# Output product of the second attention from rounded parts: three one-pass matmuls per product, in groups of two turns

## The reference, cut to what matters

```python
q, k, v = hidden @ Wq.T, hidden @ Wk.T, hidden @ Wv.T      # 32 heads of 64
q, k = apply_rope(q, k, pos, pos)
out_local  = sliding_window_attention_blockwise(q[:, :30], k[:, :30], v[:, :30], 128)
out_global = global_attention(q[:, 30:], k[:, 30:], v[:, 30:])
out = jnp.concatenate([out_local, out_global], axis=1)      # (B, L, 2048)
return jnp.einsum('blp,hp->blh', out, Wo) + bo              # Wo: 256 x 2048
```

## Time and profile before

| | |
|---|---|
| median of three runs | 3144.66 us |
| span of the profiled execution | 3149.4 us |
| second attention in it | about 1626 us to the end |
| TensorE busy over the span | 3012.4 us (96%) |
| VectorE, ScalarE, GpSimd busy | 2118.6 (67%), 1863.2 (59%), 1017.1 us (32%) |
| output product, L1961 | 1024 MATMUL rows, 241.6 us busy |
| mean granted TensorE clock | 0.987 of full speed |

### The profile page before, as it was taken

How to read it: one execution, slowest core, us unless ns; L and a number is a source line. 1 busy time by engine, 2 the same in 40 slices (tenths; PEclk the granted TensorE clock), 3 DMA queues, 4 the chain that set the end, 5 groups by cost and what they waited for, 6 DMA issues and landing times. The chain is left out here.

```text
span 3149.4 us, 66407 instructions
## 1 busy us (share of the span) xinstructions
PE 3012.4 (96%) x23638; PEld 2264.0 (72%) x23638; DVE 2118.6 (67%) x5888; ACT 1863.2 (59%) x4638; POOL 1017.1 (32%) x1627
## 2 busy tenths in 40 slices
PE   7999999999999999997988999999999999999998
PEld 5888888853444444434877888788887888788886
DVE  5666666678989989975655555655556555555556
ACT  4666666647877778773445555455554555455553
POOL 0000000001100000001016666576656666566663
PEclk9999999989999999998999999999999999999999
DMA  4111111232333232103224444344443444244432
GB/s 150 50 48 48 48 48 41 60 68 44 69 50 64 35 75 45 30 9 116 83 69 110 99 101 94 103 122 101 94 107 93 114 103 95 67 114 105 102 87 68
DMA packets 296707, 246.35 MB, mean 78 GB/s; under 512 B 149180, under 2 KB 231740, under 8 KB 296252
## 3 DMA queue, kind: packets, MB, share of 16 engines
q1 hardware_dynamic: 296380, 242.11, 31.7%
HBM read 100.71 MB, written 44.04 MB: 46 GB/s over the span
## 5 line engine op out<-in xcount | busy, mean ns | idle before, releaser
L1838 ACT ACTIVATE b_pp<-b_pp,b_nm 128x192 f32<-128x192 f32 (+2 forms) x1024 | 472.8, 463 | 447.6 <-DVE b_nm L2005 366.1
L1007 ACT ACTIVATE a_pt<-ps 128x512 f32<-128x512 f32 x1024 | 556.1, 595 | 178.9 <-PE ps L1043 177.9
L176 DVE TENSOR_REDUCE mx<-ps 128x2 f32<-128x1024 f32 x512 | 622.3, 1224 | 58.6 <-PE ps L167 44.0
L1808 POOL TENSOR_SCALAR b_pp<-b_pp,b_rc 128x192 f32<-128x192 f32 x960 | 389.2, 428 | 383.9 <-DVE b_rc L2014 383.9
L2026 DVE COPY b_pt<-ps 128x384 f32<-128x384 f32 (+2 forms) x336 | 182.1, 556 | 316.7 <-PE ps L1927 301.4
L2005 DVE CUSTOM_DVE_ANT_0 b_pp<-ps,b_mk 128x192 f32<-128x192 f32 x960 | 276.3, 354 | 136.8 <-PE ps L1906 136.8
L797 DVE SCALAR_TENSOR_TENSOR f_yac<-ps,f_cw,f_yac 128x128 f32<-128x128 f32 x992 | 278.1, 344 | 125.3 <-PE ps L596 123.0
L596 PEld LDWEIGHTS ps<-w,f_sq 128*128 128x128 f32 x2048 | 265.2, 191 | 26.5 <-issue 6.0
L596 PE MATMUL ps<-w,f_sq 128*128 128x128 f32 x2048 | 270.2, 275 | 0.3
L1961 PE MATMUL ps<-b_wo,b_oT 128*128 128x256 f32 x1024 | 241.6, 380 | 3.7 <-ACT b_vv L1831 3.7
L1056 PE MATMUL ps<-a_pt,a_v 128*32 128x256 f32 x3072 | 242.0, 395 | 0.0
(11 more groups left out here) (282 smaller groups left out, 7332.8 us busy)
## 6 DMA issues: line engine op xcount, KB each, us to landing
b_rt<-b_qf SPq DMA_DIRECT2D x1024, 64.0 KB, 2.0
qk_parts<-f_aa SPq DMA_DIRECT2D x32, 512.0 KB, 2.7
v_rows<-f_va_ SPq DMA_DIRECT2D x16, 512.0 KB, 2.8
rl<-in_W1qT SPq DMA_DIRECT2D x64, 128.0 KB, 2.6
rl<-in_W1kT SPq DMA_DIRECT2D x64, 128.0 KB, 2.7
rl<-in_W1vT SPq DMA_DIRECT2D x32, 256.0 KB, 3.2
b_wo<-in_W1oT SPq DMA_DIRECT2D x16, 512.0 KB, 4.2
b_vs<-b_vv SPq DMA_DIRECT2D x60, 128.0 KB, 2.9
```

The lines of the kernel that those rows point to most:

```text
L176: e.tensor_reduce(M["mx"][kh % 3][:, :, jt, h], P.pair(s), AX.X, ALU.max, negate=True).then_inc(P.free_sem(s), 1)
L1007: e.activation(pt[(4 * i + 2 * j + a) % 12][:, :], P.ap((*s, a)), ACT.Exp).then_inc(P.free_sem((*s, a)), 1)
L1808: m = e.tensor_scalar(x, x, r[:, 2 * u + h:2 * u + h + 1], 1.0, ALU.mult, ALU.mult)
L1838: e.activation(x, x, ACT.Exp, bias=nm[n % 4][:, c:c + 1], scale=-1.0, accum_out=sm[n % 4][:, c:c + 1]).then_inc(exp_done, 1)
```

## The change

The attention rows `oT` (fp32) are replaced by a high part `oh` (fp32r, written by ScalarE in `evac`) and a low part `ol` (fp32r, written by VectorE in the new step `evac_low`, which now frees bank 7). The output weights are loaded raw (`wr`) and split into `woh` (ScalarE) and `wol` (GpSimd) in the new step `wo_split`. A product is three fp32r matmuls by `mm3` in place of one fp32 product. A group is two turns in place of four (`PB` = 8 groups a batch), so there are 32 groups and 256 `out` steps, and two of them are taken at the end of a local stride (one after every second whole stride). All pending `store` steps are put out together, ahead of the next `out` steps. The build call also sets `dynamic_dma_scratch_size` to 1024.

```diff
             if evacs and (u == 2 or len(slots) < 3):
                 out += evacs
-                evacs = []
             if u < len(turned):
                 out.append(turned[u])
+            if evacs and (u == 2 or len(slots) < 3):
+                out += [("evac_low", f[1]) for f in evacs]
+                lowered.update(evacs)
+                evacs = []
...
-            if store:
-                p.append(store.pop())
-            if side and (not last or j % 2):
+            p += store
+            store = []
+            for _ in range(min(len(side), j % 2 if last else 2)):
                 p.append(side.pop(0))
-                if p[-1][1] % 4 == 3:
+                if p[-1][1] % PB == PB - 1:
                     store.append(("store", *p[-1][1:]))
-        if at % 4 == 3:
-            p.append(("wo", n // 4))
-            side += [("out", n // 4, t) for t in range(NQ)]
+            if at % 2 and j == 0:
+                p.append(("wo", n // 2))
+        if at % 2:
+            p.append(("wo_split", n // 2))
+            side += [("out", n // 2, t) for t in range(NQ)]
...
# sync
-                    e.dma_start(wo[n % 2][:, :, :], wo_t[:, n % 4 * 4:n % 4 * 4 + 4, :]).then_inc(wo_in[n % 2], 16)
+                    w.wait_ge(wo_low, n)
+                    e.dma_start(wr[:, :, :], wo_t[:, n % PB * 2:n % PB * 2 + 2, :]).then_inc(wo_in, 16)
...
# GpSimd
+                elif k == "wo_split":
+                    w.wait_ge(wo_high, n + 1)
+                    if n >= 2:
+                        w.wait_ge(*P.filled(("out", n - 2, NQ - 1)))
+                    e.tensor_tensor(wol[n % 2][:, :, :], wr[:, :, :], woh[n % 2][:, :, :].bitcast(F32),
+                                    ALU.subtract).then_inc(wo_low, 1)
...
# ScalarE
+                elif k == "wo_split":
+                    w.wait_ge(wo_in, 16 * (n + 1))
...
+                    e.activation(woh[n % 2][:, :, :], wr[:, :, :], ACT.Copy).then_inc(wo_high, 1)
...
-                        e.activation(oT[:, t % 8, half * CH:(half + 1) * CH], P.ap(o),
-                                     ACT.Copy).then_inc(P.free_sem(o), 1)
+                        e.activation(oh[:, t % 4, half * CH:(half + 1) * CH], P.ap(o),
+                                     ACT.Copy).then_inc(oh_ready, 1)
...
# TensorE
-                    for c in range(4):
-                        m = e.matmul(P.ap(s)[:, 0:256], oT[:, n % 2 * 4 + c, t * 128:(t + 1) * 128], wo[n % 2][:, c, :],
-                                     start=c == 0, stop=c == 3)
+                    for c in range(2):
+                        x = (slice(None), n % 2 * 2 + c, slice(t * 128, (t + 1) * 128))
+                        m = mm3(e, P.ap(s)[:, 0:256], oh[x], ol[x], woh[n % 2][:, c, :], wol[n % 2][:, c, :],
+                                c == 0, c == 1)
...
# VectorE
+                elif k == "evac_low":
...
+                        w.wait_ge(oh_ready, 2 * t + half + 1)
+                        e.tensor_tensor(ol[at], P.ap(o), oh[at].bitcast(F32), ALU.subtract).then_inc(P.free_sem(o), 1)
```

More of the change, by code:

```diff
@@ L26 @@
 ACT_TURNS = (0, 1, 2, 3)
+PB = NP // 2
 class Waits:
@@ L1503, in stride @@
                 out += evacs
-                evacs = []
             if u < len(turned):
                 out.append(turned[u])
+            if evacs and (u == 2 or len(slots) < 3):
+                out += [("evac_low", f[1]) for f in evacs]
+                lowered.update(evacs)
+                evacs = []
         out += evacs
+        out += [("evac_low", f[1]) for f in out if f[0] == "evac" and f not in lowered]
+        lowered.update(f for f in out if f[0] == "evac")
         return out
+    lowered = set()
     for n in range(NTURN):
@@ L1540, in second_attention_plan @@
         for f in fourths(at):
-            p += [f, ("evac", f[1])]
+            p += [f, ("evac", f[1]), ("evac_low", f[1])]
         if at < s:
@@ L1633, in second_attention @@
         pt = [sb(f"pt{i}", [128, 4, 128]) for i in range(5)]
-        oT = sb("oT", [128, NP // 2, L])
-        wo = [sb(f"wo{i}", [128, 4, 256]) for i in range(2)]
+        oh, ol = (sb(f"o{x}", [128, 4, L], FR) for x in "hl")
+        wr = sb("wr", [128, 2, 256])
+        woh, wol = ([sb(f"wo{x}{i}", [128, 2, 256], FR) for i in range(2)] for x in "hl")
         acc = sb("acc", [128, NQ, 256])
@@ L1646, in second_attention @@
         vb_in = [sem(f"vb_in{i}") for i in range(2)]
-        wo_in = [sem(f"wo_in{i}") for i in range(2)]
+        wo_in, wo_high, wo_low, oh_ready = sem("wo_in"), sem("wo_high"), sem("wo_low"), sem("oh_ready")
         gx_in = [sem(f"gx_in{i}") for i in range(2)]
@@ L1737, in sync @@
                 elif k == "wo":
-                    if n >= 2:
-                        w.wait_ge(*P.filled(("out", n - 2, NQ - 1)))
-                    e.dma_start(wo[n % 2][:, :, :], wo_t[:, n % 4 * 4:n % 4 * 4 + 4, :]).then_inc(wo_in[n % 2], 16)
-                    if n % 4 == 3:
+                    w.wait_ge(wo_low, n)
+                    e.dma_start(wr[:, :, :], wo_t[:, n % PB * 2:n % PB * 2 + 2, :]).then_inc(wo_in, 16)
+                    if n % PB == PB - 1:
                         for t in range(2):
-                            fetch(e, w, n // 4, t)
+                            fetch(e, w, n // PB, t)
                 elif k == "store":
-                    b, t = n // 4, s[2]
+                    b, t = n // PB, s[2]
                     r = slice(b * L + t * 128, b * L + (t + 1) * 128)
@@ L1761, in gated @@
         def gated(e, w, s):
-            b, t = s[1] // 4, s[2]
+            b, t = s[1] // PB, s[2]
             u = 8 * b + t
@@ L1793, in pool @@
                     e.tensor_tensor(y[:, t], y[:, t], rt[x % 3][:, :], ALU.add).then_inc(added[s[2]], 1)
-                elif k == "out" and n % 4 == 3 and n // 4 < B - 1:
+                elif k == "wo_split":
[4 more added lines that the diff above has]
+                                    ALU.subtract).then_inc(wo_low, 1)
+                elif k == "out" and n % PB == PB - 1 and n // PB < B - 1:
                     gated(e, w, s)
@@ L1852, in scalar @@
                         w.wait_ge(pv_done, pt_of[n, 1, pieces(n, 1) - 1] + 1 if whole(t) else pt_of[n, 3, 0] + 1)
-                        if t >= 8:
-                            w.wait_ge(*P.filled(("out", t // 4 - 2, 4 * half + 3)))
-                        e.activation(oT[:, t % 8, half * CH:(half + 1) * CH], P.ap(o),
-                                     ACT.Copy).then_inc(P.free_sem(o), 1)
+                        if t >= 4:
+                            w.wait_ge(*P.filled(("out", t // 2 - 2, 4 * half + 3)))
+                        e.activation(oh[:, t % 4, half * CH:(half + 1) * CH], P.ap(o),
+                                     ACT.Copy).then_inc(oh_ready, 1)
         def on_act(i):
@@ L2027, in vector @@
                                           P.ap(f)[:, lo:hi]).then_inc(P.free_sem(f), 1)
+                elif k == "evac_low":
+                    t, i = strides[n]
+                    if not whole(t) or i % 4 == 3:
+                        o, half = ("o", t, i // 4), i // 4
+                        at = (slice(None), t % 4, slice(half * CH, (half + 1) * CH))
+                        w.wait_ge(oh_ready, 2 * t + half + 1)
+                        e.tensor_tensor(ol[at], P.ap(o), oh[at].bitcast(F32), ALU.subtract).then_inc(P.free_sem(o), 1)
                 elif k == "out":
-                    b, g, t = n // 4, n % 4, s[2]
+                    b, g, t = n // PB, n % PB, s[2]
                     p = P.ap(s)[:, 0:256]
@@ L2037, in vector @@
                     e.tensor_tensor(acc[:, t, :], p, acc[:, t, :], ALU.add).then_inc(P.free_sem(s), 1)
-                    if n == 4 * B - 1:
+                    if n == PB * B - 1:
                         gated(e, w, s)
```

6 lines of the change are left out of this document (3 added, 3 removed).

## The result

The changed kernel takes 3222.7 us, the median of four runs, against 3144.5 us for the kernel before: a ratio of 1.0244, interval [1.0227, 1.0261]. Timed again beside seven runs of the kernel before it took 3219.3 us, ratio 1.0217 [1.0169, 1.0266]. It is slower, as forecast, but by some 75 us where 34 were forecast, and both medians lie above the range, which ends at 3205 us. (One of the first four runs took 5418 us at a mean granted clock of 0.908, the other three have a median of 3215.6 us, and all that follows is from a later profiled execution, span 3216.6 us.)

A forecast was written before the change was run, and what follows sets the result against it. TensorE was taken as the bound, with VectorE's chain at the stride's end close behind. Terms -23 + 40 + 10 + 8 - 1 = +34 us on 3144.7 gave 3179 us; range 3112 to 3205 us.

The forecast's parts named there:

- Ordinary stride: Second attention's local strides: 10.85 us becomes 10.60, `first` at about T + 2.94 (T: start of `third` 2); -23 us.
- The gate's transfers: Batches 0 to 2, last group: GpSimd waits for late-fetched gate tiles, TensorE stands nine times 4.5 us; +40 us.
- has room: `wo_split`'s extra GpSimd subtraction stands ahead of a scaling TensorE did not wait for, so it costs nothing.
- The clock: Granted clock may fall to half speed behind the twelve stalls; ends 0 and 34 us, a quarter taken, +8 us.
- Rival 3: Clock falls after nearly every stall and late rope additions hold up the next `first`: 3215 us; chance 0.12.
- The stores: At three batch changes, first outputs wait for stores put directly ahead; `proj` waits 3.4 us each; +10 us.
- The first output of a group: In local strides, nothing but VectorE's own chain was said to wait for `evac_low`; no cost for these outputs.
- Whole turns: Four single output steps replace two: -0.5 us a turn on TensorE, +1.9 on VectorE; 0 taken, ends -2 and +8.
- The tail: Last eight outputs, already bound by two `gx` buffers: only the first result comes earlier, behind `evac_low`; -1 us.

The follow-up runs named there:

- four gx buffers: Changed kernel with four gate-tile buffers instead of two, so store t fetches tile t + 4: 3151.7 us, ratio 1.0018 to the kernel before.
- the three repairs: Changed kernel with four gate-tile buffers, a semaphore for each tile's stores and each group's outputs released one stride later, together: 3135.7 us, ratio 0.9966 to the kernel before.
- stores by tile: Changed kernel with one semaphore for each tile's stores instead of one shared by parity: 3207.4 us, ratio 1.0204 to the kernel before.
- outputs a stride later: Changed kernel with each group's output steps released one stride later: 3213.2 us, ratio 1.0221 to the kernel before.
- pairs without the split: Changed kernel with fp32 operands, no `evac_low` and no `wo_split`, keeping two-turn groups and pairs of outputs and stores: 3203.6 us, ratio 1.0180 to the kernel before.

## Why the prediction was wrong

The sign, the mechanism and its place were right; the sizes of several terms were not. The largest miss is the clock's term, +8 where about 25 us were lost; the next is a wait put at nothing, `evac_low` ahead of the first outputs of a group, 12 us; the third is the gating stalls, +40 where TensorE stood 49 us.

1. *Ordinary stride, -23.* Forecast 10.60 us, measured 10.64, and `first` at T + 2.98 against T + 2.94; over 120 strides this is 1295.5 - 1276.8 = 18.7 us of gain. The matmuls themselves save less than the quarter that three passes in place of four would give by the Trainium skill (FP8 and Floating Point Precision, TensorE Precision Notes): one fp32 product takes 2 x 0.216 = 0.43 us and three fp32r matmuls 3 x 0.118 = 0.35, 18% less. The way the gain would be limited (VectorE's rope product behind `evac_low`) was shown by moving `evac_low`.
2. *The gate's transfers, +40.* This step failed together with the clock's. The late fetch, with the clock behind it, cost 60.8 to 67.6 us (four gx buffers), where these two terms gave 48. The prediction gave all nine stalls 4.5 us, from T + 12.3 less T + 7.8. Measured in batch 0: 4.10, 5.68, 7.07, and over all nine a mean of 5.4, 48.8 us in all. The first is as computed: its store is issued at T + 4.9, where T + 4.8 was taken. The third has `wo_split` ahead of the scaling, 1.24 us, which I had costed at nothing because the scaling "has room": this room was what the gating had just used up. The rest is SyncE's queue. In each second and third stall one issue takes 1.2 to 1.9 us where the others take 0.4 to 0.7; in the second of batch 0 it is a rope transfer's (1.94 us), and the store comes at T + 6.1, in the third it is that of a fetch, `b_gx<-g_rows` at 2072.28 (1.37 us). The kernel before has such long issues too (1.37 us at 2038.83), where nothing waits for them. What makes an issue long no run shows, and this split of the stalls is read from the timeline and was not tested. The 2.0 us of fixed cost that the prediction quotes from the Trainium skill (DMA: Bandwidth & Descriptors, Anatomy of one DMA) is given there for transfers that GpSimd issues; those here are SyncE's, and the sum rests on rows 8 alone.
3. *The clock, +8.* This is the largest miss. The fall came behind 11 of the 12 stalls, and 49 us of work at half clock are an estimated 25 us, near the upper bound of 34; filling the nine gating stalls gave 19.8 us of it back. A quarter of the bound was taken because one gap of 4.3 us was at hand; but that gap, too, was followed by half clock. Rival 3, with a chance of 0.12, had the fall right and its price somewhat too high.
4. *The stores, +10.* Measured 11.5 to 11.9, so the number is right, but in part by luck: TensorE stands 6.4 us at the three places and not 10, and the clock behind two of them makes up most of the rest.
5. *The first output of a group, costed at nothing.* The sentence that nothing waits for `evac_low` but the chain was wrong for one pair of outputs in each group: 28 waits and 28 strides of 11.08 us in place of 10.64, 12 us; 9.8 us by the distance of the run without it.
6. *Whole turns, taken as 0.* From the last scores ahead of the first whole turn to the first behind it: 2010.84 - 1957.22 = 53.6 us before, 2008.24 - 1953.99 = 54.3 us after. That is 2 us in all for the three whole turns in the distance, within the ends.
7. *The tail, -1.* From the last scores to the end it is 69.4 us before and after: 0.

Term by term from the trace: -18.7 for the strides, +48.8 and +6.4 of idle time, +25 for the clock, +12 for the first outputs and +2 for the whole turns are +76 us, where the distance has +73.3 and the forecast +34. By the experiments: the three repairs give back 85.1 us, and the kernel with them is 11.8 us under the kernel before, which is the 73.3. One by one the repairs give 82.1, so 3 us are left to their interplay and to the spread of single executions.

## What to carry to other kernels

When outputs are taken two at a time, everything that paced one output (the prefetch distance, buffer count, a semaphore shared by parity) is halved in time as well: ask for each transfer how long it has between its issue and its wait on the in-order queues, not in steps of the loop. A stall's price is not its idle time alone: behind stalls such as these (3.3 to 7.1 us) add what the clock takes, here some 2 us each, and charge small operations that were free elsewhere (here `wo_split`) at full price, since the room is gone. A cheaper matmul pays only as far as the next engine's order allows: the same split was worth +9.6 us of loss, 13.2 us or 23.8 us of gain, by the order around it.

## What was not expected of the hardware

- The granted clock fell to 0.50 at each of the 36 gating stalls in four of the kernels (changed, stores by tile, outputs a stride later, pairs without the split), whose idle stretches are 3.3 to 7.1 us. It may fall only when TensorE is at work again: behind 4.10, 5.68 and 7.07 us of the changed kernel it was already down, and the first three transposes took 0.90 us instead of 0.49; behind 3.74 and 4.68 us in the pairs without the split it fell 0.9 and 0.4 us after TensorE went on, and they took 0.55 and 0.59. The length of these first operations does not tell whether the clock falls.
- Stretches of about 2 us go both ways. Of the changed kernel's store stalls, 2.08 and 2.21 us were followed by half clock and 2.09 us was not.
- Keeping TensorE busy with transposes of the identity through the same waits held the mean clock at 0.98 from 2036 to 2110 us (0.84 without) and was worth 20 us of 3219.
